# Attention over a short context and its extra keys: the extra keys in two halves, and a new order of the setup

## The reference

```python
y_dca, y_main = y[:, -16:, :], y[:, :-16, :]
kv_dca = (y_dca @ Wkv_dca + bkv_dca).reshape(b, 16, 2, H, HD)      # H = 16 heads of HD = 16
k_dca  = _ln(kv_dca[:, :, 0], kn_dca_w, kn_dca_b);  v_dca = kv_dca[:, :, 1]
q      = _ln((x @ Wq + bq).reshape(b, s1, H, HD), qn_w, qn_b)       # x: after a layer norm
k, v   = per head from y_main @ Wk + bk, y_main @ Wv + bv;  k = _ln(k, kn_w, kn_b)
ctx    = softmax(q k^T / 4) v  +  softmax(q k_dca^T / 4) v_dca
x2     = x + ctx @ Wo + bo
...    # then layer norm, a router over 16 experts (2 of them for each token), a shared feed-forward part
```

## Time and profile before

| | |
|---|---|
| three runs | 529.56, 525.47, 524.77 us; median 525.47 |
| profiled execution | 524.25 us, of which the span of the trace is 522.5 us |
| TensorE busy | 478.0 us of the span (91%), granted clock 0.98 |
| VectorE, ScalarE, GpSimd busy | 342.7, 300.9, 299.4 us |
| first scores start | 44.48 us after the start of the span |

### The profile page before, as it was taken

One profiled execution on the slowest core, in us unless ns is written; L12 is line 12 of the kernel. 1 busy time (PEld: TensorE's weight loads), 2 busy tenths in 40 slices (PEclk: granted clock), 3 DMA queues, 4 the chain that ended last, 5 costly groups with the idle time before them and its releaser, 6 DMA issues.

```text
span 522.5 us, 14745 instructions
## 1 busy us (share of the span) xinstructions
PE 478.0 (91%) x5631; PEld 382.7 (73%) x5631; DVE 342.7 (66%) x805; ACT 300.9 (58%) x585; POOL 299.4 (57%) x477
## 2 busy tenths in 40 slices
PE   2887989999999999999988999989999986899995
PEld 1665778878888888887765476879899985856664
DVE  4575768868888999999887677524444444762353
ACT  2365676757778778877676623355667554443330
POOL 7025575757767677866723667666620573537570
PEclk9987998989999999999999999999999998999999
DMA  7232352333334353322200399478988895867342
GB/s 202 72 88 60 98 173 87 109 98 119 104 87 151 117 157 97 100 72 84 83 23 23 111 313 313 152 236 288 344 259 282 281 274 189 297 215 242 116 144 97
DMA packets 87928, 83.04 MB, mean 159 GB/s; under 512 B 22050, under 2 KB 80180, under 8 KB 87860
## 3 DMA queue, kind: packets, MB, share of 16 engines
q1 hardware_dynamic: 79908, 63.09, 38.5%
q0 software_dynamic: 6144, 16.79, 9.8%
q10 hardware_dynamic: 1808, 2.23, 1.3%
HBM read 39.09 MB, written 41.94 MB: 155 GB/s over the span
## 4 chain that ended last, share of the span: by engine, by line
PE 39%; DVE 5%; issue 4%; ACT 3%; another core or an unknown queue 2%; POOL 1%; ACTq 0%; DVEq 0%; POOLq 0%
PE ps L1528 8%; PE ps L1429 8%; PE ps L1437 8%; PE ps L1540 7%; PE ps L1515 3%; PE ps L1292 1%; PE ps L1308 1%; PE ps L1331 1%; ACT XN L820 1%; PE ps L1272 1%; ACTq L820 0%; ACT tile_w L820 0%; PE ps L1342 0%; DVE pmax L1654 0%
## 5 line engine op out<-in xcount | busy, mean ns | idle before, releaser
L779 POOL DMA_INDIRECT slot_x<-XN,slot_i x64 | 62.8, 981 | 32.5 <-issue 15.0
L1437 PE MATMUL ps<-sd_sb,hid 128*128 128x256 f32 x256 | 57.4, 380 | 0.7 <-issue 0.6
L1429 PE MATMUL ps<-xT_ch,su_sb 128*128 128x512 f32 x128 | 57.4, 595 | 0.0
L1437 PEld LDWEIGHTS ps<-sd_sb,hid 128*128 128x128 f32 x256 | 48.4, 190 | 10.3 <-issue 4.1
L805 POOL DMA_INDIRECT XN<-slot_y,slot_i x40 | 38.3, 958 | 28.1 <-issue 18.3
L1540 PE MATMUL ps<-down_sb,ea 128*128 x192 | 47.3, 391 | 6.0 <-DVE ea L1914 4.1
L1921 DVE COPY ey<-ps 128x512 f32<-128x512 f32 x48 | 30.9, 686 | 33.0 <-PE ps L1540 22.7
L1654 DVE TENSOR_REDUCE pmax<-ps 128x16 f32<-128x768 f32 x64 | 41.0, 682 | 9.9 <-PE ps L1272 9.6
L937 ACT ACTIVATE relu<-ps 128x512 f32<-128x512 f32 x32 | 19.0, 595 | 48.0 <-PE ps L1429 34.0
L1528 PEld LDWEIGHTS ps<-XN,tile_w 128*128 128x128 f32 x384 | 44.8, 192 | 0.9 <-issue 0.3
L1528 PE MATMUL ps<-XN,tile_w 128*128 128x128 f32 x384 | 45.1, 275 | 0.2 <-issue 0.2
(11 more groups left out here) (237 smaller groups left out, 1061.4 us busy)
## 6 DMA issues: line engine op xcount, KB each, us to landing
slot_x<-zeros SPq DMA_DIRECT2D x32, 384.0 KB, 2.9
XN<-slot_x SPq DMA_DIRECT2D x24, 512.0 KB
slot_y<-ey SPq DMA_DIRECT2D x24, 512.0 KB
x_in<-in_x SPq DMA_DIRECT2D x16, 256.0 KB, 3.0
xn2T_dram<-xn2T SPq DMA_DIRECT2D x16, 256.0 KB
xT_ch<-xn2T_dram SPq DMA_DIRECT2D x8, 512.0 KB
out<-X SPq DMA_DIRECT2D x16, 256.0 KB
y_in<-in_ctx SPq DMA_DIRECT2D x16, 128.0 KB, 2.3
```

What stands on the lines that cost most here:

```text
L779: pool.indirect_dma_start(slot_x[:, :], bass.IndirectOffsetOnAxis(ap=slot_i[:, k, t:t + 1], axis=0), XN2[:, t, :], None).then_inc(s_scat[t ...
L1429: last = pe.matmul(up_bank(c, m), su_sb[:, k, m * P:(m + 1) * P], xT_ch[:, c % 2, k, :], start=(k == 0), stop=(k == KC - 1))
L1437: last = pe.matmul(shared_out(c, t), hid[:, c % 2, m, t * P:(t + 1) * P], sd_sb[:, m, :], start=(m == 0), stop=(m == NM - 1))
```

## The change

- The extra keys are prepared in two halves (groups 0, 1 of each eight against groups 2, 3, as `t` counts them: `t` = 0, 1 and 2, 3). The first half stays in the setup. For the second half the squares go to the end of the setup, the variances behind the first `subtract_max`, the seeds into ScalarE's step 2, the Newton step and two `kn_d` products into VectorE's step 3, the transposes to the end of TensorE's step 2, and the copies into `kdT` into ScalarE's step 2, ahead of `copy_qT(1)`. They use other PSUM banks (7 and 6 in place of 4 and 5). `dca_blocks(0)` waits for two copies, `dca_blocks(1)` for four.
- `project_v(0)`, `project_k(0)`, `project_q(0)`, and the same of group 1, stand ahead of the products of the extra keys on TensorE, and `copy_k(1)` ahead of all `dca_k` on VectorE.
- Weights are centred as they come: Wq, then Wk, then both biases in one go, the extra weights after `copy_k(0)`. `bq`, `bk`, `bv` have a semaphore of their own. Only half of `bkvd` is loaded. The second y group is loaded ahead of the extra rows.
- `bias_cols` is one GpSimd instruction in place of four ScalarE ones.

The diff, cut to its core:

```diff
             def dca_blocks(g):
-                if g == 0:
-                    pool.wait_ge(d_kT, DT)
-                if g >= 2:
+                if g < 2:
+                    pool.wait_ge(d_kT, DT // 2 * (g + 1))
+                else:
                     pool.wait_ge(s_s_ps, 2 * g - 2)
...
+            def bias_columns():
+                pool.wait_ge(s_col, 1)
+                pool.tensor_tensor(bias_cols[:, :, :], zeros[:, 0:P].unsqueeze(1).to_broadcast([P, 4, P]),
+                                   ln_col[:, 6:10].unsqueeze(2).to_broadcast([P, 4, P]), ALU.add).then_inc(s_bcol, 1)
...
@@ scalar, step(i)
                 if active(i - 1):
                     copy_v(i - 1)
+                if i == 2:
+                    dca_seeds(1)
...
                 if active(i):
                     square_q(i)
+                if i == 2:
+                    copy_dca_kT(1)
                 if active(i - 1):
                     copy_qT(i - 1)
...
@@ tensor
-            def transpose_dca_k():
-                for t in range(DT):
+            def transpose_dca_k(half_no):
+                for t in range(DT // 2 * half_no, DT // 2 * (half_no + 1)):
                     pe.wait_ge(d_kn, t + 1)
...
             def scores(g, u):
                 if u == 0:
+                    if g == 0:
+                        pe.wait_ge(s_bo, 1)
+                        pe.wait_ge(d_k, 2 * DT)
+                        pe.wait_ge(d_v, 2 * DT)
                     pe.wait_ge(s_kbd, g + 1)
...
                 step(i)
+                if i == 2:
+                    transpose_dca_k(1)
...
@@ vector, step(i)
                 if active(i - 1):
                     copy_k(i - 1)
+                if i == 3:
+                    dca_normalise(1)
+                    ch.end()
                 if active(i - 3):
                     score_max(i - 3, 1)
...
+            def dca_variances(n):
+                dve.wait_ge(d_sq, n + 1)
+                cols = slice(n * DT * H, (n + 1) * DT * H)
+                ch.link(dve.tensor_reduce(rst_d[:, 3, cols], sq_d[:, n * DT:(n + 1) * DT, :]
+                                          .rearrange("p n (h d) -> p (n h) d", d=HD), AX.X, ALU.add))
...
+            def dca_normalise(n):
+                dve.wait_ge(d_seed, n + 1)
...
-            dve.wait_ge(s_wq, 16 * 3)
-            ch.need(centre(2, [heads_of(wq_sb[:, 0, :]), heads_of(wq_sb[:, 1, :]), heads_of(bq_sb[:, :])]))
+            dve.wait_ge(s_wq, 16 * 2)
+            ch.need(centre(0, [heads_of(wq_sb[:, 0, :]), heads_of(wq_sb[:, 1, :])]))
             dve.sem_inc(s_centred, 1)
-            dve.wait_ge(s_wk, 16 * 4)
-            ch.need(centre(5, [wkv_heads[:, 0, :, :], key_bias]))
+            dve.wait_ge(s_wk, 16 * 2)
+            ch.need(centre(2, [wkv_heads[:, 0, :, :]]))
             dve.sem_inc(s_centred, 1)
+            dve.wait_ge(s_wb, 16 * 3)
+            ch.need(centre(3, [heads_of(bq_sb[:, :]), key_bias]))
```

165 lines of the change are left out of this document (92 added, 73 removed).

## The result

The changed kernel takes **531.18 us** (median of four executions, 530.9 to 533.39) against 525.12 for the kernel before in the same measurement (524.08 to 529.56): ratio **1.0142**, 95% interval 1.0085 to 1.020. The forecast was 521.6 with a range of 517.8 to 526.5. The profiled execution took 531.24 us, span 529.5, against 524.25 and 522.5. In the whole document a median is of all executions, while a ratio leaves out those that took over 1.5% longer than the fastest of the same kernel, so the two can differ.

A forecast was written before the change was run, and what follows sets the result against it. TensorE was taken to bound the attention loop from step 3 on, so only the road there could shrink: 7.3 - 2.0 - 0.6 - 0.8 = 3.9 us, giving a median of 521.6 us, range 517.8 to 526.5.

The forecast's parts named there:

- First term: Setup up to the first scores of group 0: they come at 37.2 us, 7.3 us earlier (5.2 to 8.8).
- each leg: Setup: Q of group 0 copied at 16.3 to 17.4, K normalised at 22.6 to 23.7, then 14.1 us to first scores.
- Second term: Steps 2 and 3: first scores of group 0 to group 1 take 14.4 us instead of 12.43, 2.0 us given back.
- Third term: Port shared by VectorE and GpSimd: one or two instructions of the second half's normalisation lengthened by 0.5 us, 0.8 us taken.
- full exclusion at the port: Rival: VectorE lets each of three large GpSimd instructions end, losing up to 3.2 us instead of 0.8; 524.0 us, chance 0.11.
- Step 3: TensorE's bound stretch: GpSimd waits for the fourth kdT copy, delaying head variances, seeds and y copy; 0.6 us given back.
- slower: Rival: idle TensorE lets the clock fall at the start of step 3, 1.7 us, plus all low ends; 528.6 us, chance 0.06.
- I let a shift at step 3 arrive at the end whole: Everything behind step 3: follows by semaphores, not a fixed time, so the whole gain there reaches the end.
- the stall at 75.89: Rival: TensorE's unexplained 1.62 us stall in step 4 goes away with the shift, 3.3 us more gained; 518.3 us, chance 0.07.

The follow-up runs named there:

- after_whole: Changed kernel with both halves of the extra keys prepared in the setup, ahead of the first scores: median 533.34 us against 527.20 for the kernel before, ratio 0.9979.
- sets D and E: Two measurement sets on different chips, with further edits to both kernels; the kernel before has medians of 528.69 and 514.80 us there.
- after_late: Changed kernel with the second half's Newton step and products behind the maxima and subtraction on VectorE: 531.57 us against 527.20 for the kernel before, ratio 1.0071.
- before_spread: Kernel before with project_k(i) between the two halves of the probability-times-V products in each step: 533.91 us against 515.52, ratio 1.0415.
- after_pad64: Changed kernel with 64 semaphore increments in front of TensorE's first wait: 524.48 us against 515.52 for the kernel before, ratio 1.0265.
- A and C: Measurement sets: the result itself (kernel before 525.12 us), and a later one repeating both kernels, with two forms of the second half (kernel before 527.20).
- before_quiet: Kernel before with zero fills and second-norm store behind the context transposes, shared-weight loads in six parts over steps 4 to 9: 524.88 us against 528.69, ratio 0.9954.
- before_pad15: Kernel before with 15 semaphore increments in front of TensorE's first wait: 514.10 us against 514.80, ratio 0.9965.
- after_quiet: Changed kernel with zero fills, second-norm store and shared-weight loads moved away from the dense products: 527.90 us against 528.69 for the kernel before, ratio 1.0037.
- after_ref: Changed kernel, unchanged, as a reference on the same chip: 523.38 us against 514.80 for the kernel before, ratio 1.0141.
- after_minus5: Changed kernel without five TensorE waits in the setup that another wait already covers: 515.53 us against 514.80 for the kernel before, ratio 0.9894.

## Why the prediction was wrong

**First term: right, with some luck.** 7.3 us forecast, 7.1 measured; first scores at 37.39 for 37.2, and each leg within 0.5 us. Two things were not foreseen. Without the split the new order brings nothing there (`after_whole`): I had priced that half at 3.8 us, and it was 8.0. And the 44.48 that I subtracted from is a setup with a spell of low clock: the quiet and the padded kernel before of sets D and E, which have none, reach their first scores at 42.25 and 42.71, only 3.4 and 2.8 us behind the changed kernel of the same set.

**Second term: the sum was nearly right, the row that it was held against was not.** I had 14.4 us for the new step 2, and 15.2 with the port; `after_late`, without the port, has 14.97, and the changed kernel 16.74. Against the very trace that I had before me, the term and the port together took 4.3 us where I had 2.8: 0.8 of the difference is the port, 0.7 the rest of the chain. And I subtracted 12.43, a step in which TensorE ran at a clock of 0.74, as if that were the old order's length. Three of seven profiles of the old order have a clock of 0.74 to 0.76 there (12.2 to 12.4 us), one has 0.85 (11.22), and three have 1.00 and take 9.8; the two of these with the loop unchanged reach the third projection of Q at 60.7 and 61.2. The new order, with its thin TensorE between the scores, had a spell of low clock that began between 48 and 54 us in every one of the ten profiles with the split. The third projection of Q comes at 63.2 us in the mean of six profiles of the old order (60.69 to 65.56; without `before_spread`, whose step is another), and at 64.7 in five of the new one (63.98 to 65.74; without `after_pad64` with its late start). What was to be 3.9 us ahead there is 1.5 behind in these means, over different chips; inside a set it is 0.6 and 1.2 us ahead in A and C, where the old order had its low clock, and 3.6 and 4.6 behind in D and E, where `before_quiet` and `before_pad15` had none.

**Third term: mis-sized.** 0.8 us, measured 1.58. The rival "full exclusion at the port" had the mechanism right: each instruction ended behind the GpSimd instruction beside it. It cost 1.58 us and not that rival's 3.2, because VectorE had to wait for the rest of two GpSimd instructions and not for three whole ones. Moving it away made step 2 shorter by 1.4 to 1.8 us.

**Step 3.** The forecast had 0.6 us of wait, and nothing for the clock; the step took 2.2 us more. The wait was sized well: where the clock is 1.00 (`after_quiet`, `after_ref`, `after_minus5`) the changed order takes 9.15 us, 0.5 more than the 8.65 of before. The other 1.7 us are the clock, because the spell at half clock from 49.2 us ran on to 59.4. The rival "slower" named this place and this mechanism; I gave it 0.06 because all ends would have to meet. A spell of low clock between 48 and 54 us came with the split in all ten profiles, but it reached far into step 3 (clock 0.76 to 0.82) only in four of them.

**"I let a shift at step 3 arrive at the end whole": the step that failed most.** I read the stall at 75.89 as a single event that might go away, and did not ask what it was. It belongs to a series tied to every 256th instruction, with the clock behind it one costs 3 to 4 us, and any edit in front re-deals them. A lead of 0.56 us at 65 us was a loss of 7.0 at the end, and the forecast had put what happens behind 70 us at nothing. On the chip of set E, leaving out the five waits took back 7.9 of the 8.6 us by which the changed kernel was slower. The traces of the first measurement agree in size: −3.1, +3.5, +3.9 and +1.5 us of stalls and their clock make 5.8 of the 7.5 us lost behind the third projection of Q; the other 1.7 come after 300 us, and I did not trace them.

What stays open: whether it is the place of the borders that makes the changed kernel slower on average (with 5 more instructions the kernel before lost 0.4%, within its interval), and what decides when a block's packet starts, from at once to 8.8 us behind the border before it.

## What to carry to other kernels

Before a step is shortened on an engine that sets the pace, look at the clock in the row it is compared with: a stretch at half clock can be several microseconds shorter in the next execution of the same program (12.4 and 9.8 us here), and a gain counted against it is then not there. Splitting work so that it overlaps pays only where its new place is idle on the engine that it uses *and* on the one that shares its port; here putting it behind the maxima and the subtraction on VectorE made the step 1.4 to 1.8 us shorter. And where an engine with thousands of instructions is the bound, count them: stalls at equal distances in the instruction count are blocks of program landing late. What helped here was to keep large transfers away from the dense parts (0.9954 and 0.9940) and to leave out waits that others cover (7.9 us in one set). An edit should be judged on several executions and chips, since 1% either way may be the borders.

## What the runs showed of the hardware

- TensorE's program arrives in packets of 16 KB, 256 instructions; when one is late TensorE stands 0.87 to 2.30 us at that instruction. It went on 1.23 to 1.55 us after the packet had landed, in all 42 cases (271.27 against 269.96; 75.89 against 74.53; 181.49 against 180.12), and in all of them the packet had begun 1.15 us or more behind the border before.
- Behind 28 of the 42 stalls TensorE ran at 1.2 GHz for 3.4 or 6.8 us, even though it was busy throughout (4.00 of 4.00 us at 79.35).
- A semaphore increment on TensorE takes 0.15 us: 64 of them delayed its first product by 5.7 us.
- VectorE instructions of 128x64 with SBUF operands took 0.84 and 1.19 us beside GpSimd's 128x512 sums and products, and 0.21 to 0.23 alone.
- The same step of the same program took 12.43 us at a granted clock of 0.74 and 9.80 at 1.00 (`before`, and `before_spread`, in which that step is the same).
